# Most of the first turn's one-hot products moved into the stage that makes the table, with the root copies on ScalarE

## The reference

```python
def _egnn_conv(x, src, dst, edge_attr, W_msg, W_edge, W_root, b):
    msg = x[src] @ W_msg + edge_attr @ W_edge
    agg = jax.ops.segment_max(msg, dst, num_segments=x.shape[0])
    agg = jnp.where(jnp.isneginf(agg), 0.0, agg)
    return agg + x @ W_root + b
...
    c1 = jax.nn.leaky_relu(_egnn_conv(X, src, dst, edge_attr, W1_msg, W1_edge, W1_root, b1))
    c2 = jax.nn.leaky_relu(_egnn_conv(c1, src, dst, edge_attr, W2_msg, W2_edge, W2_root, b2))
```

## Time and profile before

| | us |
|---|---|
| median of 3 runs | 2301.54 (2296.12 to 2301.65) |
| the profiled execution, its own time | 2304.43 |
| its span | 2302.6 |
| mean granted TensorE clock | 0.960 of full |

### The profile page before, as it was taken

How to read it: one execution, slowest core, us unless ns; L and a number is a source line. 1 busy time by engine, 2 the same in 40 slices (tenths; PEclk the granted TensorE clock), 3 DMA queues, 4 the chain that set the end, 5 groups by cost and what they waited for, 6 DMA issues and landing times. The chain is left out here.

```text
span 2302.6 us, 57334 instructions
## 1 busy us (share of the span) xinstructions
PE 2030.8 (88%) x23524; PEld 1924.2 (84%) x23524; DVE 1240.7 (54%) x3485; ACT 672.1 (29%) x1939; POOL 759.0 (33%) x762
## 2 busy tenths in 40 slices
PE   4599688888888678888888699999999999999998
PEld 4499578777777567777777599999999999999988
DVE  8946366566565446666656474444444444444635
ACT  6824122222221212222222133332333333333434
POOL 2567366666555266656566510000000000000000
PEclk9999899999999789999999899999999999999999
DMA  3054445545554435555455400000000000000000
GB/s 75 1 164 131 106 123 137 132 132 132 131 133 117 122 87 134 134 131 133 130 132 130 126 17 2 2 2 2 2 2 2 2 2 2 1 2 2 2 2 23
DMA packets 153147, 163.58 MB, mean 71 GB/s; under 512 B 43697, under 2 KB 141612, under 8 KB 152885
## 3 DMA queue, kind: packets, MB, share of 16 engines
q1 hardware_dynamic: 100493, 83.89, 14.3%
q0 software_dynamic: 20464, 32.18, 7.5%
q10 hardware_dynamic: 31928, 43.84, 5.3%
HBM read 100.90 MB, written 58.89 MB: 69 GB/s over the span
## 5 line engine op out<-in xcount | busy, mean ns | idle before, releaser
L1473 PE MATMUL c_taken<-rows,conv_hot 125*128 125x192 f16 x6500 | 639.2, 253 | 102.7 <-issue 92.3
L1423 POOL DMA_INDIRECT conv_rows<-messages,idx_all x572 | 578.3, 1011 | 411.7 <-issue 121.6
L1473 PEld LDWEIGHTS c_taken<-rows,conv_hot 125*128 125x128 f16 x6500 | 555.7, 101 | 153.2 <-issue 137.3
L1540 DVE TENSOR_SCALAR conv_hot<-head_offset_srcs 125x640 f16<-125x640 f16 x1300 | 346.3, 328 | 272.2 <-DMA c_mask<-segment_mask 90.5
L1726 PE MATMUL l_ps<-rows,counts 125*128 125x192 f16 x5625 | 466.2, 246 | 1.9 <-DVE rows L1830 1.9
L1726 PEld LDWEIGHTS l_ps<-rows,counts 125*128 125x128 f16 x5625 | 464.0, 98 | 2.4 <-DVE rows L1830 2.4
L1726 PE MATMUL l_ps<-conv_rows,counts 125*128 125x192 f16 x5000 | 414.0, 246 | 0.8 <-DVE conv_rows L1871 0.8
L1726 PEld LDWEIGHTS l_ps<-conv_rows,counts 125*128 125x128 f16 x5000 | 412.6, 98 | 1.0 <-DVE conv_rows L1871 1.0
L1550 DVE TENSOR_TENSOR_SCAN c_scanned<-c_mask,c_scanned,c_msg 96x512 f32<-96x512 bf16 x208 | 264.5, 1272 | 151.0 <-DMA c_need<-deg 55.3
L1862 DVE SCALAR_TENSOR_TENSOR l_uf<-l_ps,l_cf,l_wide 125x96 f32<-125x96 f32 x400 | 127.1, 318 | 317.6 <-ACT l_wide L1797 317.6
L1603 ACT ACTIVATE c_back<-c_tr 128x384 f32<-128x384 f32 x208 | 102.0, 491 | 536.0 <-PE c_tr L1500 180.6
(11 more groups left out here) (297 smaller groups left out, 1774.3 us busy)
## 6 DMA issues: line engine op xcount, KB each, us to landing
running_max<-c_back ACTq DMA_DIRECT2D x208, 192.0 KB
c_attr<-attr_halves SPq DMA_DIRECT2D x412, 64.0 KB
c_mask<-segment_mask SPq DMA_DIRECT2D x206, 96.0 KB
conv_rows<-messages,idx_all POOLq DMA_INDIRECT x572
head_srcs<-sources SPq DMA_DIRECT2D x50, 160.0 KB
l0a_raw<-in_ea_t SPq DMA_DIRECT2D x50, 132.8 KB, 2.3
attr_halves<-l0a_hi SPq DMA_DIRECT2D x50, 66.4 KB, 2.1
attr_halves<-l0a_lo SPq DMA_DIRECT2D x50, 66.4 KB, 2.1
```

Of the source, the lines that this page charges most:

```text
L1423: pool.indirect_dma_start(out=gat[:, i % 2, j, :], out_offset=None, in_=c["y_d"], in_offset=bass.IndirectOffsetOnAxis(ap=idx_all[:, i * IT ...
L1473: return pe.matmul(acc[:, (NB * i + j // 2) % ACCS, j % 2 * (2 * F):(j % 2 + 1) * (2 * F)], hot[:, slot + k, j * ET:(j + 1) * ET], y[:, t, :],
L1540: last = v.tensor_scalar(hot[:, SLOTS[h % len(SLOTS)] + k, :], off[:, :], float(t * P - SRC_MID), None, ALU.is_equal)
```

## The change

- Of turn 0's eight chunks of takes, chunks 0 to 5 (90 products of 125) go into the product stage: VectorE makes their one-hots behind the batches of `HOT_BEHIND`, TensorE takes them behind those of `TAKE_BEHIND`. Chunks 6 and 7 stay at the start of the edge stage. Turn 0 uses three slots of the ring, clear of the root term.
- Turn 1's chunks 0 and 1 are taken before turn 0's first message group, where they stood behind it.
- The bias is a row of the weights, against a row of ones beneath the turned state; so the root term is a plain copy, done by ScalarE (`root_of`), no longer VectorE.
- The accumulators of the takes are now there in the product stage, which leaves it two banks for turning (three before) and three for products (four before, one of the three borrowed from the takes' accumulators). A bank is free when its root copy is done. The turned state is a ring of three blocks of three tiles, no longer whole.
- Turn 1's gathers wait by `room(0, j)`, as those of turn 2 do, in place of `behind_first_takes(j)`.
- `head.vector` (three small operations on the edge weights) goes from batch 3 to the end of the product stage; the 16 warming products at its end are gone. The sources are offset by ScalarE as before, for turn 0 behind batch 0.

```diff
+FIRST_SLOTS = 3
+HOT_BEHIND = {1: 0, 3: 1, 5: 2, 6: 3, 8: 4, 10: 5}
+TAKE_BEHIND = {3: 0, 5: 1, 7: 2, 8: 3, 10: 4, 12: 5}
+BLK_W2 = 3
+XT_BLOCKS = 3
...
-        pt = st.enter_context(nc.psum_tensor(f"{tag}_pt", [128, 3, BANK], F32))
-        py = st.enter_context(nc.psum_tensor(f"{tag}_py", [128, 4, BANK], F32))
+        pts, pys = (2, 3) if w2 else (3, 4)
+        pt = st.enter_context(nc.psum_tensor(f"{tag}_pt", [128, pts, BANK], F32))
+        py = st.enter_context(nc.psum_tensor(f"{tag}_py", [128, 2 if w2 else 4, BANK], F32))
...
-                    if b >= 4:
-                        pe.wait_ge(s_o, b - 3)
+                    if b >= pys:
+                        pe.wait_ge(s_root if w2 else s_o, b - pys + 1)
...
+                    if w2 and b in TAKE_BEHIND:
+                        h = TAKE_BEHIND[b]
+                        pe.wait_ge(s_o, CHUNKS[h][-1] // per + 1)
+                        head.take(pe, 0, h, y)
...
+                    def root_of(b):
+                        r = batches[b]
+                        act.wait_ge(s_o, b + 1)
+                        act.activation(root[:, r.start:r.stop, :], of(r, slice(F, m)), ACT.Copy).then_inc(s_root, 1)
...
                         act.activation(y[:, r.start:r.stop, 0:F], of(r, slice(0, F)), ACT.Copy, scale=YS).then_inc(s_hi, 1)
-                        if b >= 2 and left[0][1] <= batches[b - 2].stop:
+                        if b == 0:
+                            head.offset_srcs(act, 0)
+                        else:
+                            root_of(b - 1)
+                        if b >= 3 and left[0][1] <= batches[b - 3].stop:
                             park(*left.pop(0))
...
-                        v.tensor_tensor(root[:, r.start:r.stop, :], of(r, slice(F, m)),
-                                        b_row[:, :].unsqueeze(1).to_broadcast([P, len(r), F]), ALU.add).then_inc(s_o, 1)
+                        if b in HOT_BEHIND:
+                            head.one_hots(v, 0, HOT_BEHIND[b])
...
                             if i == 1:
-                                behind_first_takes(j)
+                                room(0, j)
...
-                takes(0, *range(NC))
+                takes(0, *range(IN_PRODUCT, NC))
                 for i in range(N_IT):
+                    if i == 0:
+                        takes(1, 0, 1)
                     messages(i, 0)
-                    takes(i + 1, 0, 1)
+                    if i:
+                        takes(i + 1, 0, 1)
```

234 lines of the change are left out of this document (126 added, 108 removed).

## The result

The changed kernel takes 2307.55 us (median of 20 runs), the kernel before beside it 2301.6 (20 runs): a ratio of 1.0029, 95% interval 1.0019 to 1.004. The profiled execution took 2310.94 us and its span is 2309.0. All ratios in this document leave out three executions on chip 13 that ran at a granted clock of 0.83, 0.75 and 0.37 (2303 and 2546 us of the kernel before, 6991 us of `n1`).

A forecast was written before the change was run, and what follows sets the result against it. TensorE was taken to set the loop's pace, entering it late through thin stretches. Gains of 11.4 and 12.5 us, less 6 for arrears, made 17.9: 2304.4 to 2286.5, less 2.9 for the median, 2283.5 us (2268 to 2300).

The forecast's parts named there:

- Product stage: Stage ahead of the edge stage: 75 takes ahead of the last product lengthen it by 6.4 and 4 us.
- ScalarE, VectorE, GpSimd's fill: Product stage: ScalarE's root copies no bound, VectorE's work even, GpSimd's fill ahead of first use, at most 0.5 us.
- First gather at L+3.9: Start of the edge stage: the first gather stays 3.9 us after L.
- L: End of a convolution's last product work on VectorE; 252.3 and 799.4 us in the kernel before.
- Third group at L+23.5: Turn 0's third message group starts 23.5 us after L, before 41.3 and 40.0; 23.9 us gained together.
- What is late next: Early turns: no group waits for data, but unbroken gather streams cost TensorE 3 us (0 to 11) a convolution, 6 in all.
- new thin stretches in turns 1 to 3: Sign of being wrong: turns 1 to 3 of the edge stage hold thin stretches that were not there before.
- thin stretches: Early edge stage: TensorE works only 5.5 of 19.4 and 4.9 of 16.0 us, paired with unbroken streams of gathers.
- The thin stretches come back: Rival, no change: two more short stretches of 5.4 us in each convolution, 22 us, give 2299.5; 11 in 100.
- GpSimd's arrears bind: Rival, slower: turn 2's gathers begin 9 and 7 us later, 16 us slower, 2317.5; 12 in 100.
- The slowness goes along with the takes: Rival, no change: slowness is in the takes' instruction supply; 19 us turn up in the product stage, 2301; 3 in 100.

The follow-up runs named there:

- n1: Kernel before, with all 286 gathers of each convolution as plain loads of other rows from GpSimd's queue: 2031.82 us, ratio 0.9973 (chip 13).
- n3: Changed kernel, with every turn's gathers from turn 1 on held to the turn before: 2055.93 us, ratio 1.0089 (chip 13).
- h1: Changed kernel as it is, run on chip 8: 2053.75 us, ratio 1.0076.
- k1: Changed kernel, with the row of ones and the bias row's zeros written by VectorE instead of GpSimd: 2045.41 us, ratio 1.0042 (chip 12).
- h3: Changed kernel, with every turn's gathers from turn 1 on held to the turn before: 2057.37 us, ratio 1.0103 (chip 8).
- h4: Changed kernel, with all gathers as plain loads of other rows from GpSimd's queue: 2027.47 us, ratio 0.9959 (chip 8).
- k3: Kernel before, with TensorE's first product also waiting for a signal in GpSimd's queue, without the fill: 2038.72 us, ratio 1.0008 (chip 12).
- e3_before_one_turn_ahead: Kernel before, with gathers of turns 2 and later held to the turn before: 2044.41 us, ratio 1.0033 (chip 11).

## Why the prediction was wrong

Predicted was 2283.5 us (2268 to 2300), measured 2307.55.

*Product stage: right.* TensorE is busy 19.2 of 20.8 us. The extension was predicted at 6.4 and 4 us and measured at 5.0 and 3.2.

*ScalarE, VectorE, GpSimd's fill: right on that chip, wrong as a rule.* I had bounded the fill by 0.5 us and looked for its first use, and not past the queue that it stands in. On chips 8 and 11, and in `n3` on chip 13, TensorE's first product of the second convolution waits for it, and from `h1` to `k1` it was worth about 7 us.

*First gather at L+3.9: right* (L+3.5 and L+4.1).

*Third group at L+23.5: right* (L+24.5 and L+23.6), with some luck: the first message group, which I had at L+10 to 12, began at L+15.3 and L+18.3.

*What is late next: this is the step that failed.* I charged 3 us (0 to 11) a convolution for GpSimd's arrears, because an unbroken stream had cost 5.4 us in the earlier trace rows. Behind the third group, from where that term counts, the changed kernel lost 16.2 and 15.5 us (480.2 us to the last message where it was 464.0, and 479.7 where it was 464.3). The stretch of turn 1 was no short one of 4.3 us for 1.6 of work, but one of 19 us for 7.7 and one of 32 us for 15.6. Turn 2's gathers found their waits met, as I wrote, and streamed, as I wrote, in streams of 14 and 23; I then sized their price by the shortest example that the trace had, though the long one, 19.4 us beside a stream of 18 gathers, stood right next to it. My own sign of being wrong, new thin stretches in turns 1 to 3, came in both convolutions. The other terms together were right: at the third group the changed kernel was 25.0 us ahead (11.8 and 13.2), where I had 23.9. With 31.6 us in place of the 6 the sum is 2304.4 - 25.0 + 31.6 = 2311.0, and the profiled execution took 2310.9. That this sum closes is bookkeeping; it says where the time went and not why.

*The rivals.* "The thin stretches come back" had the right mechanism at 11 in 100, and the wrong size: 22 us in all, by stretches of 5.4 each. "GpSimd's arrears bind" would have had turn 2's gathers at 297.8; they began at 293.4 (288.8 in the kernel before), found no wait, and were all issued by 306.9, 18.5 us before group 0 of turn 2. So no message waited for them; the time went in the thin stretch beside them. "The slowness goes along with the takes" did not come: the product stage took its takes dense, and in the second convolution's thin stretch message products come as thinly as takes (a row is shown in the last section).

*A better first look.* The gather-to-end times, 501.4 and 500.7 us, were in the trace of before, and I did not form them. I measured from L to the third group, a place from which the gain could still be taken back. That both convolutions need the same time from the first gather on, though their first message groups stand 29.6 and 28.1 us behind it, does not prove a bound, but it asks the right question: which work between the first gather and the end gets shorter, if takes leave turn 0?

*What stays open.* Why the first chip has thin stretches, and so what made the step fail there. The runs that were to tell gathers and instruction supply apart (`h3`, `h4`, `n1` to `n3`) came on chips without them. Gather streams by themselves are not enough: on chips 8, 11, 12 and 13 they stand as close, and TensorE is busy nearly without a break beside them. The traces hold one thing against the supply of instructions: the queue for instructions moved no packet between 262.4 and 281.8 us in the kernel before and between 291 and 310 in the changed one, so it was not a packet on its way in that queue that held TensorE up inside these stretches. Why gather-to-end is the same for both kernels on the first chip, to 1.5 us, is not shown either; GpSimd's unbroken queue, the reason on the others, does not hold there.

## What to carry to other kernels

Work taken off the front of a pipeline is worth only what the end of the pipeline gives back. Before counting the gain at the first group, measure from the event that the change does not move, or moves later (here the first gather), to the last instruction, and look for an engine that never finds a closed wait in between, however idle its share of busy time looks (GpSimd is busy 36% of the span in `k3`). Whatever stands ahead of that event can then be paid in full, here up to 7 us a stage. A fill that nobody seems to wait for takes the place of its queue: look at what is ahead of it on that engine in the second pass of the loop, not in the first. And size the price of a stall by the example in the trace that is nearest in length, here the long one.

## What was unexpected of the hardware

The same kernel takes 2301.6 us (20 runs) on the first chip and 2036 to 2038 us on each of four others, 13% apart, at nearly the same mean granted clock (0.960 and 0.981 to 0.989). The difference is in the edge convolutions. A turn takes 18.7 us in the mean on the one and 14.3 on the others. By the pages of the profile TensorE is busy 2030.8 us on the one and 1934.2 in `e3_before_one_turn_ahead`, 97 us less for the same work, and idle 272 us against 113. A change tuned to the stretches of one chip finds none of them on another.

In a thin stretch of the first chip TensorE's takes come in groups of one to four, and in the long stretches shown here they became dense again within 5 us of the end of a stream of gathers. Message products are thin there too. From 851.7 to 860.8 us of the changed kernel's second convolution single products of messages and takes start in steps of about 0.7, 1.4 or 2.1 us, with no named cause. One of them:

```profile
854.51 0.27 PE L1542 MATMUL c_msg<-ident,conv_rows 128*96 128x128 f16 x1 [1.82 <-issue]
```

VectorE was idle in these stretches as well, for 10.2 us at one time in the kernel before, and for 8.4 and 17.1 us in the changed one.

The window of the same 19 us on chip 8 with the same kernel, 15 gathers in it:

```profile
291.00:310.00 19.00, 19.00 (x239) 18.43 (x237) 15.80 (x41) 5.81 (x11) 14.53 (x15) 1.00 0.65 168
```

TensorE is busy for all of it, where it worked 7.7 us on the first.
